# A gated linear attention layer whose step runs scores, transposes, context and then the projections on TensorE, with queries scaled on Pool and 64x64 score blocks

## What is computed

```python
def _gla(h, Wq, Wk, Wv, Wg, Wo):
    B, T, _ = h.shape
    q = _l2norm((h @ Wq).reshape(B, T, N_HEADS, D_K))
    k = _l2norm((h @ Wk).reshape(B, T, N_HEADS, D_K))
    v = (h @ Wv).reshape(B, T, N_HEADS, D_V)
    alpha = jax.nn.sigmoid(h @ Wg).reshape(B, T, N_HEADS, D_K)

    def step(S, inp):
        a_t, k_t, v_t, q_t = inp
        S = a_t[..., None] * S + k_t[..., None] * v_t[..., None, :]
        o_t = jnp.einsum('bhkv,bhk->bhv', S, q_t)
        return (S, o_t)
...
    return o @ Wo
```

## Time and profile before

| | us |
|---|---|
| median of 3 runs | 2826.84 |
| their range | 2822.14 to 2827.99 |
| span of the profiled execution | 2826.2 |

### The profile page before, as it was taken

One profiled execution on the slowest core, in us unless ns is written; L12 is line 12 of the kernel. 1 busy time (PEld: TensorE's weight loads), 2 busy tenths in 40 slices (PEclk: granted clock), 3 DMA queues, 4 the chain that ended last, 5 costly groups with the idle time before them and its releaser, 6 DMA issues. The chain is left out here.

```text
span 2826.2 us, 46612 instructions
## 1 busy us (share of the span) xinstructions
PE 2198.0 (78%) x15104; PEld 1519.0 (54%) x15104; DVE 1816.6 (64%) x4918; ACT 1290.3 (46%) x2801; POOL 1179.0 (42%) x1150
## 2 busy tenths in 40 slices
PE   2799999999998679329479997959999999952780
PEld 0466666666666557317345554845566666541560
DVE  3677777687775767301367774649888888857113
ACT  1445454544543227313335564736666666620223
POOL 1424233342421100545422221558777787710663
PEclk9899999999999759569779997969999999965885
DMA  6400000000002000012333332000000000000113
GB/s 197 104 1 0 0 0 0 0 0 0 0 0 68 0 0 0 31 54 67 89 90 90 85 83 79 0 1 1 0 0 0 0 0 0 0 30 0 43 42 94
DMA packets 103412, 88.55 MB, mean 31 GB/s; under 512 B 12060, under 2 KB 90166, under 8 KB 103222
## 3 DMA queue, kind: packets, MB, share of 16 engines
q1 hardware_dynamic: 96150, 72.67, 9.5%
q0 software_dynamic: 7168, 14.73, 1.7%
HBM read 59.02 MB, written 40.96 MB: 35 GB/s over the span
## 5 line engine op out<-in xcount | busy, mean ns | idle before, releaser
L3278 POOL TENSOR_SCALAR mb_w<-mb_duT,mb_bT 128x256 f32<-128x256 f32 x512 | 468.0, 933 | 118.0 <-PE bank L3288 81.6
L3213 DVE TENSOR_TENSOR_SCAN mb_hs<-mb_dA,bank 128x512 f32<-128x512 f32 x256 | 300.9, 1205 | 35.9 <-issue 25.0
L38 POOL TENSOR_TENSOR scrap<-ones 128x1 f32<-128x1 f32 x64 | 12.5, 195 | 695.9 <-DVE gla_ss L421 488.6
L3307 PE MATMUL bank<-mb_hc,ident 128*128 128x512 f32 x512 | 257.7, 627 | 15.6 <-DVE mb_hc L3223 15.3
L3269 ACT ACTIVATE mb_dA<-mb_delta,mb_A 128x255 f32<-128x255 f32 x512 | 216.6, 495 | 9.2 <-DVE mb_hs L3213 9.1
L2435 DVE TENSOR_REDUCE ra_mx<-bank 128x2 f32<-128x512 f32 x256 | 163.9, 686 | 61.3 <-PE bank L2289 58.7
L2017 ACT ACTIVATE e_hid<-bank,e_b 128x512 f32<-128x512 f32 (+1 forms) x128 | 79.6, 634 | 258.5 <-PE bank L2061 191.4
L2525 ACT ACTIVATE ra_pT<-bank 128x512 f32<-128x512 f32 x256 | 141.2, 600 | 114.3 <-PE bank L2311 114.0
L3288 PE MATMUL bank<-ident,mb_w 128*128 128x128 f32 x1024 | 149.9, 280 | 34.3 <-DVE mb_hs L3213 26.3
L3223 DVE TENSOR_TENSOR mb_hc<-mb_hs,bank 128x1024 f32<-128x1024 f32 x128 | 153.0, 1195 | 0.0
L2096 DVE TENSOR_TENSOR e_y<-bank,e_b 128x512 f32<-128x512 f32 (+1 forms) x32 | 20.0, 625 | 197.8 <-PE bank L2071 120.2
(11 more groups left out here) (552 smaller groups left out, 5917.1 us busy)
## 6 DMA issues: line engine op xcount, KB each, us to landing
results<-const_empty SPq DMA_DIRECT2D x2, 4096.0 KB
e_got<-results SPq DMA_DIRECT2D x32, 256.0 KB, 3.3
rope_rows<-ra_part SPq DMA_DIRECT2D x48, 128.0 KB, 1.9
ra_k<-rope_rows SPq DMA_DIRECT2D x32, 192.0 KB, 3.3
ra_q<-rope_rows SPq DMA_DIRECT2D x32, 192.0 KB, 4.3
queue<-const_spare_rows SPq DMA_DIRECT2D x1, 4128.0 KB
e_x<-queue SPq DMA_DIRECT2D x8, 516.0 KB
e_w<-in_L_ffn_w SPq DMA_DIRECT2D x2, 2048.0 KB, 8.2
```

Source lines behind the costliest of these rows:

```text
L3213: dve.tensor_tensor_scan(hs[n // 2 % 2][:, n % 2, :, :].rearrange("p c t -> p (c t)"), dA[n % RD][:, :, :].rearrange("p c t -> p (c t)"), ...
L3278: ins = pool.tensor_scalar(w[n % RH][:, h, :], duT[k][:, h, :], bT[k][:, h, n:n + 1], None, ALU.mult)
L3307: ins = pe.matmul(YB[:, :], g.ident[:, :], hc[grp % 2][:, j, :, :].rearrange("p c t -> p (c t)"), start=(n == 0), stop=(n == NS - 1))
```

## The change

The way of scaling queries, the form of the score blocks, the table of items and the order of the pieces within a step all change.

- Pool multiplies the raw queries by their norms in place, four heads first and then twelve (`scaled_queries`). The parts, their transposition, the spread matmul, the ScalarE copy of it and VectorE's scaling go; ScalarE copies the context out of PSUM instead (`act_context`).
- `pe_scores` computes the diagonal 64x64 blocks of each tile (eight matmuls) instead of whole 128x128 ones (four). The two conditional copies of 128x384 become one of 128x768, and the six multiplies of `dve_factors` three.
- |z| is made by ScalarE (Abs), and VectorE makes the minimum alone.
- `PLAN` puts `y` and `h` in step 0, then `k`, `q`, `z`, `v`. A result `y` is three sequences late, not two (`LAG`), with two buffers of `oT`. There are two buffers of squares.
- Within a step TensorE runs scores of pair `n - 1`, then `pe_project` of `n`, then context of `n - 2`, then all items. VectorE runs the factors of `n`, the first item, `dve_seen` of `n - 1`, the other items. ScalarE runs exponentials, items, the context copy.

```diff
-    PLAN = {0: ("", "", "h"), 1: ("z0", "z1", "z2"), 2: ("y", "z3", "k0"), 3: ("k1", "k2", "k3"),
-            4: ("q0", "q1", "q2"), 5: ("q3", "v0", "v1"), 6: ("v2", "", "v3"), 7: ("", "", "r")}
-    ORDER = [item for step in range(HP) for item in PLAN[step] if item]
+    PLAN = {0: ("y", "h"), 1: ("k0", "k1", "k2"), 2: ("k3", "q0", "q1"), 3: ("q2", "q3"), 4: ("z0", "z1"), 5: ("z2", "z3"),
+            6: ("v0", "v1"), 7: ("v2", "v3")}
+    ORDER = [item for step in range(HP) for item in PLAN[step]]
+    LAG = 3
...
         if kind == "z":
-            act.wait_ge(z_ready, s * 4 + (c + 1))
+            act.wait_ge(z_psum, s * 4 + (c + 1))
+            act.activation(chunk_out(az, c), PB[:, :], ACT.Abs).then_inc(za_ready, 1)
+            act.wait_ge(za_ready, s * 4 + (c + 1))
             act.activation(chunk_out(az, c), chunk_out(az, c), ACT.Exp, scale=-1.0).then_inc(ze_ready, 1)
...
         pe.wait_ge(qkx_ready, at(s, hp))
         if hp >= 1 or not first(s):
-            pe.wait_ge(sc_ready, 2 * at(s, hp - 1))
+            pe.wait_ge(sc_ready, at(s, hp - 1))
+        for hd, r in enumerate(HALVES):
+            pe.matmul(SC[:, hd, 2 * P:3 * P], f128[b][r, 0, :], f128[b][r, 1, :], start=True, stop=True)
+        for t in range(2):
+            for part in HALVES:
+                for hd, r in enumerate(HALVES):
+                    pe.matmul(SC[part, hd, t * P + part.start:t * P + part.stop], km[r, t, part], qm[r, t, part],
+                              start=True, stop=True)
         for t in range(2):
             for hd, r in enumerate(HALVES):
-                pe.matmul(SC[hd][:, t * P:(t + 1) * P], km[b][r, t, :], qm[b][r, t, :], start=True, stop=True)
-        for hd, r in enumerate(HALVES):
-            pe.matmul(SC[hd][:, 2 * P:3 * P], k128[b][r, :], q128[b][r, :], start=True, stop=True)
-        for t in range(2):
-            for hd, r in enumerate(HALVES):
-                ins = pe.matmul(SC[hd][0:64, t * P + 64:(t + 1) * P], k64[b][r, t, :], q64[b][r, t, :],
+                ins = pe.matmul(SC[0:64, hd, t * P + 64:(t + 1) * P], f64[b][r, 0, t, :], f64[b][r, 1, t, :],
                                 start=True, stop=True)
         ins.then_inc(s_psum, 1)
...
-        for hd in range(2):
-            dve.copy_predicated(sT[b][:, hd, :], g.seen[:, :], SC[hd][:, 0:3 * P]).then_inc(sc_ready, 1)
-
-    def dve_scale(dve, s, hp):
-        dve.wait_ge(rb_ready, at(s, hp))
-        dve.tensor_tensor(oT[:, hp, :], OB[:, 0:256], rb[:, :], ALU.mult).then_inc(o_ready, 1)
...
+        dve.copy_predicated(sT[b][:, :, :], g.seen[:, :].unsqueeze(1).broadcast_to([P, 2, 3 * P]), SC)\
+            .then_inc(sc_ready, 1)
...
+    def pe_body(pe, s, k, nxt, step):
+        if over(s, step, 1):
+            sb_, _, hb = back(s, k, step, 1)
+            pe_scores(pe, sb_, hb)
+        if s is not None:
+            pe_project(pe, s, k, step)
+        if over(s, step, 2):
+            pe_context(pe, *back(s, k, step, 2))
+        for item in items_of(nxt, step):
...
+    def dve_body(dve, s, k, nxt, step):
+        items = items_of(nxt, step)
+        if s is not None:
+            dve_factors(dve, s, step)
+        if step == 0 and not (isinstance(nxt, int) and nxt == NSEQ):
+            dve_tokens(dve, nxt)
+        for n, item in enumerate(items):
+            if n == 1 and over(s, step, 1):
+                sb_, _, hb = back(s, k, step, 1)
+                dve_seen(dve, sb_, hb)
...
+                dve_item(dve, nxt, 1 - k, item)
+        if len(items) < 2 and over(s, step, 1):
+            sb_, _, hb = back(s, k, step, 1)
+            dve_seen(dve, sb_, hb)
...
+            def scaled_queries(s, k):
+                pool.wait_ge(rnq_ready, s + 1)
+                for heads in (slice(0, 4), slice(4, HEADS)):
+                    n = heads.stop - heads.start
+                    rows = tok["q"][k][:, :, heads.start * DK:heads.stop * DK].rearrange("p t (h d) -> p t h d", d=DK)
+                    pool.tensor_tensor(rows, rows, rnq[:, :, heads].unsqueeze(3).broadcast_to([P, 2, n, DK]), ALU.mult)\
+                        .then_inc(qs_ready, 1)
```

More of the change, by code:

```diff
@@ L287, in gla @@
     prep, zeroed, later_loaded = sig("prep"), sig("zeroed"), sig("loads")
[L288 to L294, removed]
+    names = ["hn", "hp", "h", "zp", "zm", "za", "ze", "zl", "lna", "kp", "qp", "sq", "ss", "bound", "rnk", "rnq", "vp", "v",
+             "ktok", "qtok", "qs", "qkp", "ep", "ex", "mid", "qkx", "sp", "sc", "op", "o", "yp", "y"]
@@ L398, in act_item @@
+            if not first(s) or n >= 2:
+                act.wait_ge(ss_ready, n - 1)
             act.wait_ge(copied[kind], s * 4 + (c + 1))
[L399 to L405 removed]
+            act.activation(sq[c % 2][:, :], part, ACT.Square).then_inc(sq_ready, 1)
@@ L600, in none, with nothing, in_steps @@
-    def none(*args):
-        pass
+        dve.copy_predicated(sT[b][:, :, :], g.seen[:, :].unsqueeze(1).broadcast_to([P, 2, 3 * P]), SC)\
+            .then_inc(sc_ready, 1)
+    def nothing(*args):
+        pass
+    def in_steps(eng, body, end):
+        for step in range(HP):
+            body(eng, None, 1, 0, step)
+        for s in range(LAG):
+            for step in range(HP):
+                body(eng, s, s % 2, s + 1, step)
+        with eng.Fori(0, (NSEQ - 1 - LAG) // 2) as i:
+            for j in range(2):
+                for step in range(HP):
+                    body(eng, i * 2 + (LAG + j), (LAG + j) % 2, i * 2 + (LAG + j + 1), step)
+        for step in range(HP):
+            body(eng, NSEQ - 1, 1, NSEQ, step)
+        end(eng)
@@ new lines, in over, with back, items_of, result_of @@
+    def over(s, step, n):
+        return s is not None and (step >= n or not first(s))
+    def back(s, k, step, n):
+        return (s, k, step - n) if step >= n else (s - 1, 1 - k, HP + step - n)
+    def items_of(nxt, step):
+        if isinstance(nxt, int) and nxt == NSEQ:
+            return {0: ("y",), 4: ("y",)}.get(step, ())
+        return PLAN[step]
+    def result_of(nxt, step):
+        return NSEQ + 1 if step and isinstance(nxt, int) and nxt == NSEQ else nxt
+    def pe_body(pe, s, k, nxt, step):
[7 more added lines that the diff above has]
+        for item in items_of(nxt, step):
+            if isinstance(nxt, int) and nxt == NSEQ and step:
+                pe.wait_ge(y_ready, NSEQ - 2)
+                pe_result(pe, NSEQ - 2, k ^ 1, bank_of("y"))
+            else:
+                pe_item(pe, nxt, 1 - k, item)
@@ new lines, in pe_end, with act_body @@
+    def pe_end(pe):
+        s = NSEQ - 1
+        pe_scores(pe, s, HP - 1)
+        pe_context(pe, s, 1, HP - 2)
+        pe_context(pe, s, 1, HP - 1)
+        pe.wait_ge(y_ready, s)
+        pe_result(pe, s, 1, bank_of("y"))
+    def act_body(act, s, k, nxt, step):
+        if s is not None:
+            act_exponentials(act, s, step)
+        for item in items_of(nxt, step):
+            act_item(act, nxt, 1 - k, item)
+        if over(s, step, 2):
+            act_context(act, *back(s, k, step, 2))
```

293 lines of the change are left out of this document (108 added, 185 removed).

## The result

The changed kernel takes 3023.2 us (median of 4 runs, 3021.1 to 3032.4), the kernel before, run beside it, 2827.4: a ratio of 1.070, 95% interval 1.068 to 1.072. The span of the profiled execution, the slowest of the four, is 3030.6 against 2826.2, so 204 us longer, where the medians lie 196 apart. The forecast was 3003 with a range of 2948 to 3070: the sign and the range held, the forecast itself is 20 us short.

The account below looks back on a forecast made before the run. TensorE set the pace before, a closed ring of waits after: 15 sequences +168, two passes without a result -3.5, last pass +16.5, start -4.5, total +176 on 2826.84, so 3003 us; range 2948 to 3070.

Parts of the forecast that it names:

- The ring: Each step: scores, transposes, context, first projection, ScalarE, VectorE, conditional copy, next scores close a circle; 60.3 us a sequence against 49.09.
- k/q step: Steps 1, 2, 3 (keys and queries): the circle of waits takes 7.55 us; TensorE idles 1.4 and 2.3.
- S: TensorE's score matmuls of a step: 1.24 us before, taken as 1.46 after, or 1.08.
- tile rival: Score matmuls: the four 64x64 array tiles run fully beside each other, S 0.38 us shorter; 2960 us, chance 0.25.
- steps 5 and 6: Steps with gate chunks and the logarithm on ScalarE, priced together: 15.69 us of the sequence.
- Pool's work: Pool's added query scaling, some 4.5 us, bounds 4.5 and 9: covered in the steady part, costing only past some 25.
- step 0: The step with result y: 8.62 us, since VectorE waits for the whole result before the conditional copy.
- clock rival: TensorE falls to 1.2 GHz in one step per sequence: 15 x 4.5 plus the last pass, +93; 3096 us, chance 0.14.
- The start: Up to the first gate sums, keys projected first: 85.5 against 90.50, -4.5 us, between -6 and +1.
- two passes without a result: Two passes that make no y: 1.7 us less each, -3.5 us.
- The last pass: The final pass, without preparation: 59.2 us against 42.7, so +16.5.
- Not the ring (2762): Rival: TensorE's own work still bounds, a sequence of 42.7 to 45.8 us and about 2 more; 2762 us, chance 0.03.

Follow-up runs that it names:

- e7: Changed kernel with VectorE's conditional copy first in the step and ScalarE's context copy ahead of the projections; 2816.8 us, 0.9974 of the kernel before.
- u2: Changed kernel with the old TensorE order and ScalarE's logarithm moved behind the exponentials of step 6; 2728.2 us, 0.9658 of the kernel before.
- s1: Changed kernel with its eight 64x64 score matmuls put back to four of 64x128; 3084.8 us, 1.0928 of the kernel before.
- e2: Changed kernel with VectorE's conditional copy first in the step, ahead of the factors; 2829.4 us, 1.0026 of the kernel before.

## Why the prediction was right, point by point

**The ring: right, but for one term.** Each link of a k/q step is within 0.06 of its price, save S. 7.55 was forecast, 7.15 measured; S is 0.43 shorter, and the other links are 0.03 longer in sum. The wait at the scores is 1.44 and 2.30 where 1.4 and 2.3 stood in the text. The two order runs show that the order makes the loss: alone it costs 9.2%, and without it the other parts gain 1.2%.

**S: mis-sized, 1.03 for 1.46.** The eight new matmuls take 0.28, not 0.76; the first two take 0.42, not 0.32. I read 47 ns per record of the earlier trace rows's L483 as a rate of issue. The sixteen records of L451 take 0.28 until L455 starts, 17.5 ns each, so it wasn't. The four of L455 (eight records) still take 0.33: they write the first 64 rows of the bank only, so they use one half of the array's columns, and eight matmuls on both halves take no longer than these four on one. That is the tile rival. What is over 0.28 in the 0.33 may lie in the change to full-size transposes; no run tests it. The tile rival had S right (1.08), and its sentence from the Trainium skill (TensorEngine Tiling (Array Packing), section Tiling Modes: four independent tiles) agrees with this trace. The other sentence, a floor of about 25 ns between starts (the Trainium skill, TensorE: Matmul & The Clock Gate, section "Wait — 56ns, not 53.3ns?"), is not what these records show: 17.5 ns. Taking S alone, the forecast would have been 2960.

**The two things that filled the gap.** 60.3 a sequence was forecast. Less 7 x 0.43 for S it is 57.3 (S counts once for steps 5 and 6 together). Pool holding L508 adds 1.47 in step 6, which was not in the working at all: I had called Pool's work covered, and looked only at who waits for Pool's results. The clock in step 7 adds 2.4 (8.5 for 6.1), and step 0 is 0.2 over its price: 61.4, as measured. So the sum came out near by errors against each other, -3.0 for S and +3.9 for the hold and the clock. That is luck: over 15 sequences they are 45 and 58 us.

**The clock rival** came true in part, in a milder form than its 4.5 a sequence: the half clock covered most of one step, 2.4. It was there after 3.77, a wait that I had put at about 2, since Pool's hold was missing from it.

**The ends.** The start gained 7.8, not 4.5 (first gate sums at 82.72 for 90.50); the terms of the text add up to 85.5, which is 5.0 and not 4.5, Pool's power for the keys began at 62.96, not 65, and its scaling took 3.76, not 4.5. The 3.5 us for two passes without a result didn't come: the first such step takes 6.53 for 8.38, but the step behind it 9.97 for 7.16. The last pass lost 24.3, not 16.5: from 1003.96 to 1070.94 it is 67.0 for 42.7. Its scores wait up to 2.56 each. Without a result to make, only the first step and the one behind the last result take 5.5, which is the text's 5.84 less 0.43 for S; the others take 6.3 to 7.0, at a granted clock of 0.74 to 0.76 (1016.68 to 1030.70 and 1051.80 to 1058.77):

```profile
1011.18 0.49 PE L447 MATMUL bank<-gla_f 64*128 64x128 f32 x4 [1.53 <-DVE gla_sT L518]
1016.68 0.49 PE L447 MATMUL bank<-gla_f 64*128 64x128 f32 x4 [2.56 <-DVE gla_sT L518]
...
1051.80 0.80 PE L447 MATMUL bank<-gla_f 64*128 64x128 f32 x4 [2.56 <-DVE gla_sT L518]
1058.77 0.80 PE L447 MATMUL bank<-gla_f 64*128 64x128 f32 x4 [2.56 <-DVE gla_sT L518]
```

The account in the spans: -7.8 at the start, +185.6 for the 15 bodies (736.1 to 921.7, from the first gate sums to those of the last pass), +24.3 for the last pass, +2.3 behind the layer: 204.4. The text had -4.5, +164.5 and +16.5.

**Not the ring (2762)** did not happen. The runs with the old order come near its number, 2792, and 2728 with the logarithm moved. TensorE's own work of 42.7 a sequence, which the text had with S at 1.08, is the 42.2 of the last kernel.

## What to carry to other kernels

With one buffer between a producer and a consumer, trace the whole circle through every in-order queue before moving one piece: here the cost was a sum on VectorE that stood ahead of the copy, harmless while its input came first. Break such a ring where a piece waits that doesn't need what stands ahead of it, and put a long instruction (a logarithm with its two table loads) behind the short one that others wait for. And look at what runs beside a slow engine's long instruction, not only at who needs its result.

## What was not expected of the hardware

- VectorE's multiplication of two SBUF operands ended only 0.3 us behind Pool's subtraction or scaling: 1.89 for 0.42, 2.98 for 0.42 in e7. Shorter Pool instructions in direct succession held two of them. Beside Pool's power of 128x32, 5.46 us long, it kept its 0.42.
- Sixteen records of 64x64 f32 matmuls in 0.28 us, in either order of the halves, where eight of 64x128 in the same place take 0.57 (412.67 to 413.24).
- TensorE at 1.2 GHz after each wait of 3.76 in the changed kernel, but after waits of 2.3 only at times. In the two runs without the fall in step 7, or with less of it, the clock fell more often in step 4.
- A gap of about 2 us on TensorE, without a releaser, where the loop comes round. It shows in u2, s1 and e2, and not in the changed kernel.
